# Attention and experts on one core: the last 1024 queries in two groups of 512 instead of four of 256

## The chip, the core and the metric

The kernel runs on one core of a Trainium2 chip. Its engines work side by side, each through its own instruction stream in order, and meet only at semaphores: TensorE (PE, with its weight loads as PEld), VectorE (DVE), ScalarE (ACT), GpSimd (POOL) and SyncE (SP), which starts most DMAs. The metric is the device time of one execution in microseconds (us). A profiled execution also has a span, from its first to its last recorded work.

## The reference

```python
x = L0_attn_x                                   # (1, 2048, 128)
xn = _layernorm(x, axis=-1)
x = x + attention(xn) + ffn(xn)
# attention: one softmax(q k^T * scale) v over all 2048 keys, then a projection
qkv = jnp.einsum('bse,he->bsh', x, w_qkv); q, k, v = jnp.split(qkv, 3, axis=-1)
probs = jax.nn.softmax(jnp.einsum('bqh,bkh->bqk', q, k) * scale, axis=-1)
out = jnp.einsum('bqk,bkh->bqh', probs, v)      # then swapaxes, reshape, w_proj, + b_proj
# ffn: 8 experts (128 -> 512 -> 128), each token in its best two
topv, topi = jax.lax.top_k(softmax(t @ W_gate + b_gate), 2)
mid = relu(einsum('nd,edh->neh', t, W1) + b1); eout = einsum('neh,ehd->ned', mid, W2) + b2
out = einsum('ne,ned->nd', route, eout) @ W_out + b_out
```

## The kernel before, in words

The 2048 tokens stand on 128 partitions as 16 tiles of 128. Attention goes by **groups** of queries (`GROUPS`), here eight of 256. A group goes through the 16 tiles of keys in **steps**. A step fills one bank of PSUM, 512 columns of scores: with 256 queries that is two tiles of keys (`CH` = 2) and 8 steps to a group. With 512 queries it would be one tile of keys and 16 steps, by the same functions.

In a step, PE makes `scores` (each product as three fp32r matmuls, high and low parts), ACT takes the exponential (L454; from group 4 on also an fp32r copy, L453, whose remainder DVE makes, `low`, L611), and two steps later PE sums the values (`values`: L917 in plain fp32 in groups 0 to 3, L926, L927 and L930 as three fp32r products from group 4 on).

The exponentials need each query's maximum first. While one group runs, PE makes the **pairs** of the next group: `pair(g, m)` (L853) is two matmuls of 512 columns for a tile of 128 queries and half of the keys. DVE reduces each to a maximum (`pair_max`, L601, 128x1024 elements). A group has two pairs for each tile of 128 queries. All pairs from group 1 on write the same two banks, so each waits until DVE has read the one before it (`max_read`). `PAIR_STEP[g]` lists the steps of group g at which the pairs of group g+1 stand. If a step has several, the first goes ahead of the step's `values` and the others behind them. When all are read, `row_max` (L606) joins them, and ahead of the group's last step `max_row` (L861) turns them into a row on PE, one transpose for each tile of queries. `q_project` makes the next group's queries in step 0.

After a group, ACT copies the sum out (`copy_u`, L461), and PE and DVE finish it in **rounds** of 256 queries: `out_rows` (L947), `scale_out` (L617, L620), `project` (L961), then one `add_out` for the whole group (L628). `out_rows` of a round waits for the `scale_out` of the one before it, since both use the same bank.

Groups 0 to 3 (`PRE` = 4) run ahead of the **experts**, a loop over 39 tiles of sorted tokens (L1025, L1037, L1051 on PE; L343 on POOL), whose outputs go to `slots_out` in memory. The pairs of group 4 are made in group 3, ahead of the experts. Group 4 and those behind it run after the experts. Beside them POOL gathers the experts' outputs: for each of the 16 tiles of tokens two indirect DMAs (L380) and a multiplication (`weigh`, L375). DVE's `combine(j)` (L756) waits for both and stands at a fixed step s counted from the experts' end (4 + 13(j+1)/8, so j = 15 at s = 30). At s = 14, 22, 26 and 31 (`BLOCK_AT`) PE turns four combined tiles (`moe_transpose`, L1081), and a step later multiplies them with W_out (`moe_project`, L1089); DVE adds that in `moe_add` (L763).

Behind the last step PE has the last `values`, the last `moe_project` and the last group's rounds. SP stores the output in pieces (L277), each when all that is added to its rows is there.

Of the kernel before, what the change touches and what calls it, by code (L numbers as in the profile page):

```python
# [12 lines left out]
def attention_moe_kernel(nc, x, w_qkv, w_proj, b_proj, w_in, b_in, w_gate, b_gate,  # L13
# [4 lines left out]
    P = 128  # L18
    S, D = x.shape[1], x.shape[2]
    NT = S // P  # L20
    NE, _, DM = w1.shape
    HC = DM // P
    BK = 512
    NR = S // BK
    TB = BK // P
# [10 lines left out]

    GROUPS = [(256 * g, 256) for g in range(8)]
    PRE = 4  # L40
    WHOLE = 4

    PAIR_STEP = [[4, 5, 5, 6]] + 6 * [[1, 2, 4, 5]] + [[]]
    NG = len(GROUPS)
    SIZE = [n for _, n in GROUPS]
    CH = [BK // n for n in SIZE]
    STEPS = [NT // c for c in CH]
# [21 lines left out]
    def pairs_at(g, k):  # L69
        return [m for m, at in enumerate(PAIR_STEP[g]) if at == k]  # L70

# [8 lines left out]
    with ctx:  # L80
# [143 lines left out]
        def _(sp):  # L224
# [45 lines left out]
                store_y(t)  # L270

            ov = out.rearrange("o (p j) e -> p (o j) e", p=P)
            cuts = [TB * r for r in range(NR)] + [GROUPS[NG - 1][0] // P, NT]
            for a, b in zip(cuts, cuts[1:]):
                sp.wait_ge(Z["moe_added"], (b - 1) // TB + 1)
                sp.wait_ge(Z["x_added"], sum(q < P * b for q, _ in GROUPS))
                sp.dma_start(ov[:, a:b, :], x_sb[:, a:b, :]).then_inc(Z["stored"], 16)  # L277
            sp.wait_ge(Z["stored"], 16 * (NR + 1))

        @block.gpsimd  # L280
        def _(pool):
# [51 lines left out]
            def load_experts(first, n):  # L333
                _, values = nc.values_load_multi_w_load_instructions(
                    texp[0:1, first:first + n], engines=[pool.engine], min_val=0, max_val=NE - 1,
                    skip_runtime_bounds_check_because="a count of experts that is clamped to the last one")
                experts.update({first + k: v for k, v in enumerate(values)})
# [190 lines left out]
        def _(dve):  # L528
# [69 lines left out]
            def pair_max(g, m):  # L598
                b = pair_bank(g, m)
                dve.wait_ge(Z["max_done"], FIRST_PAIR[g] + m + 1)  # L600
                dve.tensor_reduce(part_max[:, g % 2, m // 2, m % 2:m % 2 + 1], ps[:, b:b + 2, :], AX.XY,  # L601
                                  ALU.max).then_inc(Z["max_read"], 1)

            def row_max(g):
                dve.wait_ge(Z["max_read"], FIRST_PAIR[g + 1])
                dve.tensor_reduce(neg_max[:, g % 2, 0:TILES[g]], part_max[:, g % 2, 0:TILES[g], :], AX.X, ALU.max,  # L606
                                  negate=True).then_inc(Z["neg_max_ready"], 1)
# [15 lines left out]
            def add_out(g):  # L623
                first = GROUPS[g][0] // P
                at = x_sb[:, first:first + TILES[g], :]
                dve.wait_ge(Z["proj_done"], FIRST_ROUND[g + 1])
                dve.wait_ge(Z["x_biased"], 1 + first + TILES[g])
                return dve.tensor_tensor(at, ps[:, MB, 0:SIZE[g]].rearrange("p (j e) -> p j e", e=D), at, ALU.add)  # L628
# [77 lines left out]
            for g in range(PRE):  # L706
                for k in range(STEPS[g]):
                    for m in pairs_at(g, k):
                        pair_max(g + 1, m)
                    if k == PAIR_STEP[g][-1]:  # L710
                        row_max(g + 1)
# [47 lines left out]
            def moe_add(b):  # L759
                at = x_sb[:, TB * b:TB * (b + 1), :]  # L760
                dve.wait_ge(Z["wo_done"], b + 1)
                dve.wait_ge(Z["x_added"], min(NG - 1, sum(q < BK * (b + 1) for q, _ in GROUPS)))
                dve.tensor_tensor(at, ps[:, MX + 1, :].rearrange("p (j e) -> p j e", e=D), at, ALU.add).then_inc(Z["moe_added"], 1)  # L763

            for g in range(PRE, NG):
                for k in range(STEPS[g]):
                    i = FIRST[g] + k
                    s = i - BASE_B
                    for m in pairs_at(g, k):
                        pair_max(g + 1, m)  # L770
                    if g + 1 < NG and k == PAIR_STEP[g][-1]:
                        row_max(g + 1)
# [16 lines left out]
        def _(pe):  # L789
# [287 lines left out]
            def moe_transpose(b, pairs):  # L1077
                pe.wait_ge(Z["c_ready"], TB * (b + 1))
                pe.wait_ge(Z["max_read"], pairs)
                for j in range(TB):  # L1080
                    last = pe.transpose(ps[:, MX, P * j:P * (j + 1)], z[:, TB * b + j, 0, :], ident[:, 0:P])  # L1081
                last.then_inc(Z["cT_done"], 1)
# [9 lines left out]
            for g in range(PRE, NG):  # L1092
                for k in range(STEPS[g]):
# [9 lines left out]
                    if s in BLOCK_AT:  # L1103
                        moe_transpose(BLOCK_AT[s], FIRST_PAIR[g + 1] + sum(at <= k for at in PAIR_STEP[g]))
                    if s - 1 in BLOCK_AT:
# [40 lines left out]
```

## Time and profile before

| | before |
|---|---|
| median of 3 runs | 242.5 us (242.16 to 242.7) |
| profiled execution, its own time | 242.35 us |
| its span | 240.6 us |
| TensorE (PE) busy | 226.1 us, 94% |
| VectorE busy | 136.6 us, 57% |
| ScalarE busy | 111.7 us, 46% |
| GpSimd busy | 140.9 us, 59% |
| granted TensorE clock, mean | 0.998 |

The profiled execution took 1.75 us more than its span, and 0.15 us less than the median of the runs. Shares of busy time are means over parts with different limits, so the table alone doesn't tell what a change in one part is worth. The clock is given as a share of full speed. In the rows further down, a time in square brackets is how long the engine had been idle before the instruction, with what ended the wait.

### The profile page before, as it was taken

The numbers are of one execution on the slowest core, as the hardware profiler recorded it, in microseconds if no ns is written. First come the engines' busy times: TensorE is split into PE (matmuls) and PEld (weight loads), VectorE is DVE, ScalarE is ACT, GpSimd is POOL, SyncE is SP. The second block draws the span as 40 slices with busy tenths as digits, with TensorE's granted clock in tenths as the row PEclk, the third lists the DMA queues.
The fourth block names the chain that finished last, engine by engine and source line by source line (L and its number), as shares of the span: only waits on it lengthen the run. The fifth ranks groups of instructions, "written<-read, shape, count | busy, mean of one in ns | idle before, by whom it ended". The sixth has DMA issues, their size and how long they took to land.

```text
span 240.6 us, 4828 instructions
## 1 busy us (share of the span) xinstructions
PE 226.1 (94%) x1724; PEld 214.0 (89%) x1724; DVE 136.6 (57%) x330; ACT 111.7 (46%) x265; POOL 140.9 (59%) x163
## 2 busy tenths in 40 slices
PE   7699977999999999899999999999899999999983
PEld 7688865889999998899999999999899899999983
DVE  4978585364252551445444445444677886985642
ACT  2572520433524325354444554444656656567561
POOL 3149007888888820266555666553088888888610
PEclk9999999999999999999999999999999999999999
DMA  6799911101111121022222222221111113113201
GB/s 180 282 324 341 322 31 46 45 33 46 46 41 39 43 66 44 14 55 76 70 73 71 67 71 75 69 75 38 33 46 34 44 35 82 40 40 83 75 15 44
DMA packets 23047, 19.54 MB, mean 81 GB/s; under 512 B 3280, under 2 KB 19696, under 8 KB 22768
## 3 DMA queue, kind: packets, MB, share of 16 engines
q1 hardware_dynamic: 20000, 14.71, 20.1%
q0 software_dynamic: 2048, 4.20, 6.5%
q10 hardware_dynamic: 976, 0.33, 0.5%
q8 instruction: 14, 0.23, 0.4%
q14 instruction: 9, 0.07, 0.1%
HBM read 10.97 MB, written 8.26 MB: 80 GB/s over the span
## 4 chain that ended last, share of the span: by engine, by line
PE 78%; DVE 8%; DMA 4%; POOL 3%; issue 2%; ACT 1%; ACTq 1%; POOLq 0%; DVEq 0%
PE ps L1051 15%; PE ps L1037 15%; PE ps L917 10%; PE ps L853 6%; PE ps L792 5%; PE ps L793 5%; PE ps L794 5%; DVE part_max L601 3%; PE ps L926 2%; POOL wtab L380 2%; PE ps L930 2%; PE ps L927 2%; DMA w_raw<-in_L_attn_w_proj_dram 2%; PE ps L1025 2%; PE ps L800 2%
## 5 line engine op out<-in xcount | busy, mean ns | idle before, releaser
L343 POOL COPY wst<-wtab 128x1156 f32 x39 | 45.0, 1154 | 39.3 <-DVE y_sb L738 39.3
L454 ACT ACTIVATE pf<-ps 128x512 f32<-128x512 f32 x64 | 38.1, 595 | 36.5 <-PE ps L794 36.1
L601 DVE TENSOR_REDUCE part_max<-ps 128x1 f32<-128x1024 f32 x32 | 38.9, 1223 | 13.3 <-PE ps L853 13.1
L380 POOL DMA_INDIRECT wtab<-slots_out,slots x32 | 34.4, 1074 | 15.9 <-DMA slots_out<-y_sb 8.4
L353 POOL DMA_INDIRECT slots_in<-hl,slots x32 | 31.5, 985 | 18.7 <-DVE slots L677 11.7
L730 DVE TENSOR_SCALAR mid<-ps,wst 128x128 f32<-128x128 f32 x78 | 23.8, 347 | 32.5 <-PE ps L1037 32.5
L1051 PE MATMUL ps<-wst,mid 128*128 128x128 f32 x312 | 41.3, 275 | 0.7 <-DVE x_sb L628 0.7
L792 PE MATMUL ps<-q_hi,xnT_hi 128*128 128x256 f32 x128 | 41.2, 322 | 0.5 <-ACT q_hi L439 0.5
L1037 PE MATMUL ps<-xgT,wst 128*128 128x128 f32 x312 | 41.3, 275 | 0.0
L1051 PEld LDWEIGHTS ps<-wst,mid 128*128 128x128 f32 x312 | 38.0, 192 | 0.8 <-ACT mid L494 0.8
L1037 PEld LDWEIGHTS ps<-xgT,wst 128*128 128x128 f32 x312 | 38.0, 192 | 0.1
L793 PE MATMUL ps<-q_hi,xnT_lo 128*128 128x256 f32 x128 | 36.1, 282 | 0.0
L794 PE MATMUL ps<-q_lo,xnT_hi 128*128 128x256 f32 x128 | 36.0, 281 | 0.0
L917 PE MATMUL ps<-pf,xn 128*128 128x256 f32 x128 | 32.7, 379 | 0.0
L453 ACT ACTIVATE ph<-ps 128x512 fp32r<-128x512 f32 x32 | 19.1, 598 | 23.4 <-PE ps L794 23.1
L611 DVE TENSOR_TENSOR pl<-pf,ph 128x512 fp32r<-128x512 f32 x32 | 22.6, 706 | 12.2 <-ACT pf L454 12.2
L494 ACT ACTIVATE mid<-ps,wst 128x128 f32<-128x128 f32 x78 | 24.4, 364 | 7.5 <-PE ps L1037 7.5
L917 PEld LDWEIGHTS ps<-pf,xn 128*128 128x128 f32 x128 | 23.0, 189 | 3.1
L487 ACT ACTIVATE xgT<-ps 128x128 f32<-128x128 f32 x39 | 10.9, 278 | 31.8 <-PE ps L1025 31.8
L792 PEld LDWEIGHTS ps<-q_hi,xnT_hi 128*128 128x128 f32 x128 | 24.3, 190 | 1.3 <-ACT q_hi L439 0.7
L853 PE MATMUL ps<-xnT_hi,q_hi 128*128 128x512 f32 x64 | 21.2, 416 | 4.3 <-DVE part_max L601 3.8
L793 PEld LDWEIGHTS ps<-q_hi,xnT_lo 128*128 128x128 f32 x128 | 24.3, 190 | 0.6
(145 smaller groups left out, 341.4 us busy)
## 6 DMA issues: line engine op xcount, KB each, us to landing
wtab<-in_L_ffn_W_dram SPq DMA_DIRECT2D x16, 256.0 KB, 5.9
xg<-slots_in SPq DMA_DIRECT2D x39, 64.0 KB, 2.0
slots_out<-y_sb SPq DMA_DIRECT2D x39, 64.0 KB, 1.5
slots_in<-wst SPq DMA_DIRECT2D x2, 1024.0 KB, 5.0
x_sb<-in_L_attn_x_dram SPq DMA_DIRECT2D x4, 256.0 KB, 4.9
out_dram<-x_sb SPq DMA_DIRECT2D x3, 256.0 KB, 2.6
wtab<-in_L_ffn_b_dram SPq DMA_DIRECT2D x1, 512.0 KB, 7.4
slots_in<-hl,slots POOLq DMA_INDIRECT x32
```

The source lines that it names most:

```text
L343: pool.tensor_copy(wst[:, t % 4, :], wtab[:, bass.ds(experts[t], 1), :].rearrange("p a n -> p (a n)")).then_inc(Z["staged"], 1)
L353: pool.indirect_dma_start(out=slots_in, out_offset=bass.IndirectOffsetOnAxis(ap=slots[:, c, j:j + 1], axis=0), in_=hl[:, j, 0:D], in_offse ...
L380: pool.indirect_dma_start(out=z[:, j, c, :], out_offset=None, in_=slots_out, in_offset=bass.IndirectOffsetOnAxis(ap=slots[:, c, j:j + 1], ...
L454: act.activation(pf[:, i % 3, :], ps[:, st_bank(i), :], ACT.Exp).then_inc(Z["pf_done"], 1)
L601: dve.tensor_reduce(part_max[:, g % 2, m // 2, m % 2:m % 2 + 1], ps[:, b:b + 2, :], AX.XY, ALU.max).then_inc(Z["max_read"], 1)
L792: pe.matmul(dst, lh, rh, start=start, stop=False)
L793: pe.matmul(dst, ll, rh, start=False, stop=False)
L794: return pe.matmul(dst, lh, rl, start=False, stop=stop)
L853: last = pe.matmul(ps[:, pair_bank(g, m) + b, :], q_hi[:, g % 2, P * t:P * (t + 1)], xnT_hi[:, at:at + BK], start=True, stop=True)
L917: last = pe.matmul(dst, xn[:, c, :], pf[:, i % 3, cols(g, h)], start=(first and h == 0), stop=(final and h == CH[g] - 1))
L1037: last = pe.matmul(ps[:, 2 * (t % 2) + h, SL * (c % 2):SL * (c % 2 + 1)], wst[:, t % 4, P * c:P * (c + 1)], xgT[:, t % 2, :], start=True, ...
L1051: last = pe.matmul(ps[:, y_bank(t), 0:D], mid[:, t % 2, c, :], wst[:, t % 4, DM + D * c:DM + D * (c + 1)], start=(c == 0), stop=(c == HC - 1))
```

## The change

The four groups of 256 behind the experts become two of 512. Groups 4 and 5 then have one tile of keys to a step, 16 steps, eight pairs and two rounds each. Group 4's eight pairs stand in group 3's eight steps, ahead of the experts, where four stood. Group 5's eight stand in group 4. The output is stored in four pieces of 512 rows, where the last 512 rows were two pieces.

```diff
-    GROUPS = [(256 * g, 256) for g in range(8)]
+    GROUPS = [(256 * g, 256) for g in range(4)] + [(1024, 512), (1536, 512)]
     PRE = 4
     WHOLE = 4
 
-    PAIR_STEP = [[4, 5, 5, 6]] + 6 * [[1, 2, 4, 5]] + [[]]
+    PAIR_STEP = [[4, 5, 5, 6]] + 2 * [[1, 2, 4, 5]] + [[1, 2, 2, 3, 4, 4, 5, 6], [1, 3, 5, 6, 8, 9, 11, 12], []]
```
```diff
-            cuts = [TB * r for r in range(NR)] + [GROUPS[NG - 1][0] // P, NT]
+            cuts = [TB * r for r in range(NR + 1)]
             for a, b in zip(cuts, cuts[1:]):
                 sp.wait_ge(Z["moe_added"], (b - 1) // TB + 1)
                 sp.wait_ge(Z["x_added"], sum(q < P * b for q, _ in GROUPS))
                 sp.dma_start(ov[:, a:b, :], x_sb[:, a:b, :]).then_inc(Z["stored"], 16)
-            sp.wait_ge(Z["stored"], 16 * (NR + 1))
+            sp.wait_ge(Z["stored"], 16 * NR)
```

First place: PE in group 3, from the pair at step 2 on. L853 is a pair, L917 the values, L947 `out_rows`, L792 to L794 the scores. Before:

```order
L853 MATMUL ps<-xnT_hi,q_hi 128x512 x2
L917 MATMUL ps<-pf,xn 128x256 x2
L947 MATMUL ps<-wvT,ut 128x130 x2
L792 MATMUL ps<-q_hi,xnT_hi 128x256
L793 MATMUL ps<-q_hi,xnT_lo 128x256
L794 MATMUL ps<-q_lo,xnT_hi 128x256
L792 MATMUL ps<-q_hi,xnT_hi 128x256
L793 MATMUL ps<-q_hi,xnT_lo 128x256
L794 MATMUL ps<-q_lo,xnT_hi 128x256
L917 MATMUL ps<-pf,xn 128x256 x2
L961 MATMUL ps<-wpT,o_sb 128x128 x2
```

The same place now:

```order
L853 MATMUL ps<-xnT_hi,q_hi 128x512 x2
L917 MATMUL ps<-pf,xn 128x256 x2
L853 MATMUL ps<-xnT_hi,q_hi 128x512 x2
L947 MATMUL ps<-wvT,ut 128x130 x2
L792 MATMUL ps<-q_hi,xnT_hi 128x256
L793 MATMUL ps<-q_hi,xnT_lo 128x256
L794 MATMUL ps<-q_lo,xnT_hi 128x256
L792 MATMUL ps<-q_hi,xnT_hi 128x256
L793 MATMUL ps<-q_hi,xnT_lo 128x256
L794 MATMUL ps<-q_lo,xnT_hi 128x256
L853 MATMUL ps<-xnT_hi,q_hi 128x512 x2
L917 MATMUL ps<-pf,xn 128x256 x2
```

A second pair stands behind the values of step 2, and one more in step 3.

Second place: PE's last instructions, from the last steps' values on. Before:

```order
L926 MATMUL ps<-ph,xn_hi 128x256
L927 MATMUL ps<-ph,xn_lo 128x256
L926 MATMUL ps<-ph,xn_hi 128x256
L927 MATMUL ps<-ph,xn_lo 128x256
L930 MATMUL ps<-pl,xn_hi 128x256 x2
L1089 MATMUL ps<-wo_sb,cT 128x128 x4
L947 MATMUL ps<-wvT,ut 128x130 x2
L961 MATMUL ps<-wpT,o_sb 128x128 x2
```

Now:

```order
L926 MATMUL ps<-ph,xn_hi 128x512
L927 MATMUL ps<-ph,xn_lo 128x512
L930 MATMUL ps<-pl,xn_hi 128x512
L1089 MATMUL ps<-wo_sb,cT 128x128 x4
L947 MATMUL ps<-wvT,ut 128x130 x2
L961 MATMUL ps<-wpT,o_sb 128x128 x2
L947 MATMUL ps<-wvT,ut 128x130 x2
L961 MATMUL ps<-wpT,o_sb 128x128 x2
```

A step's values are three matmuls of 512 columns instead of six of 256, and the last group has two rounds.

Third place: DVE's last instructions, from the last `combine` (L756) on. Now:

```order
L756 SCALAR_TENSOR_TENSOR wtab<-wtab,gate 128x128
L611 TENSOR_TENSOR pl<-pf,ph 128x512
L763 TENSOR_TENSOR x_sb<-ps,x_sb 128x512
L617 RECIPROCAL rinv<-ps 128x2
L620 TENSOR_TENSOR o_sb<-ps,rinv 128x256
L617 RECIPROCAL rinv<-ps 128x2
L620 TENSOR_TENSOR o_sb<-ps,rinv 128x256
L628 TENSOR_TENSOR x_sb<-ps,x_sb 128x512
```

Before, L617 and L620 stood there once and L628 had 128x256 elements. POOL's instructions are the same, in the same order.

## Rows read from the trace of the kernel before

**Rows 1.** The page: the chain that ended last, by engine.
```profile
PE 78%; DVE 8%; DMA 4%; POOL 3%; issue 2%; ACT 1%; ACTq 1%; POOLq 0%; DVEq 0%
```
**Rows 2.** Windows (us: busy us and count by engine, clock, DMA, GB/s), group 3.
```profile
77.32:92.56 15.24, 15.24 (x97) 13.96 (x96) 6.50 (x9) 6.05 (x11) 7.46 (x8) 1.00 0.21 61
```
**Rows 3.** Timeline of PE in group 3: start us, length us, instruction.
```profile
79.15 0.28 PE L794 MATMUL ps<-q_lo,xnT_hi 128*128 128x256 f32 x1
79.27 0.62 PE L853 MATMUL ps<-xnT_hi,q_hi 128*128 128x512 f32 x2
79.73 1.02 PE L917 MATMUL ps<-pf,xn 128*128 128x256 f32 x4
...
81.30 0.64 PE L853 MATMUL ps<-xnT_hi,q_hi 128*128 128x512 f32 x2
...
84.66 0.61 PE L961 MATMUL ps<-wpT,o_sb 128*128 128x128 f32 x4
85.02 0.36 PE L792 MATMUL ps<-q_hi,xnT_hi 128*128 128x256 f32 x1
...
85.81 0.62 PE L853 MATMUL ps<-xnT_hi,q_hi 128*128 128x512 f32 x2
...
87.85 0.64 PE L853 MATMUL ps<-xnT_hi,q_hi 128*128 128x512 f32 x2
...
90.76 0.38 PE L861 MATMUL ps<-ident,neg_max 128*128 128x128 f32 x2
...
92.56 0.27 PE L1025 MATMUL ps<-ident,xg 128*128 128x128 f32 x1
```
**Rows 4.** Timeline of DVE in group 3.
```profile
79.93 1.23 DVE L601 TENSOR_REDUCE part_max<-ps 128x1 f32<-128x1024 f32 x1 [1.08 <-PE ps L853]
...
89.78 0.16 DVE L606 TENSOR_REDUCE neg_max<-part_max 128x2 f32<-128x4 f32 x1
```
**Rows 5.** Timeline of POOL behind the experts: first gather, three later ones, last weigh.
```profile
173.99 1.47 POOL L380 DMA_INDIRECT wtab<-slots_out,slots  x1 [8.37 <-DMA slots_out<-y_sb]
...
187.34 1.00 POOL L380 DMA_INDIRECT wtab<-slots_out,slots  x1 [0.17 <-issue]
...
190.44 1.00 POOL L380 DMA_INDIRECT wtab<-slots_out,slots  x1 [0.17 <-issue]
...
197.45 1.46 POOL L380 DMA_INDIRECT wtab<-slots_out,slots  x1 [0.17 <-issue]
...
228.58 0.60 POOL L375 TENSOR_SCALAR wtab<-wtab,gate 128x128 f32<-128x128 f32 x1 [1.10 <-DMA wtab<-slots_out,slots]
```
**Rows 6.** Timeline of DVE behind the experts.
```profile
187.28 0.39 DVE L756 SCALAR_TENSOR_TENSOR wtab<-wtab,gate 128x128 f32<-128x128 f32 x1 [0.25 <-POOL wtab L375]
...
197.36 0.68 DVE L611 TENSOR_TENSOR pl<-pf,ph 128x512 fp32r<-128x512 f32 x1
...
231.51 0.34 DVE L756 SCALAR_TENSOR_TENSOR wtab<-wtab,gate 128x128 f32<-128x128 f32 x1
```
**Rows 7.** Waits from 169 us on: engine, line, releaser: total us, times, longest.
```profile
PE ps L853 <- DVE part_max L601: 1.1, 2, 0.6
```
**Rows 8.** Timeline of PE and DVE at the end.
```profile
235.44 0.68 PE L947 MATMUL ps<-wvT,ut 128*128 128x130 f32 x4
235.64 0.69 DVE L763 TENSOR_TENSOR x_sb<-ps,x_sb 128x512 f32<-128x512 f32 x1 [2.61 <-PE ps L1089]
...
236.92 0.71 PE L961 MATMUL ps<-wpT,o_sb 128*128 128x128 f32 x4 [0.80 <-DVE o_sb L620]
237.72 0.42 DVE L628 TENSOR_TENSOR x_sb<-ps,x_sb 128x256 f32<-128x256 f32 x1 [0.86 <-PE ps L961]
```
**Rows 9.** All copies of line 461: ns min/median/max, first and last start.
```profile
L461 ACT ACTIVATE ut<-ps x8: 603/618/634, 48.6 to 234.7; 128x256 f32<-128x256 f32 x8
```
**Rows 10.** DMA issues: KB each, median us to landing.
```profile
out_dram<-x_sb SPq DMA_DIRECT2D x3, 256.0 KB, 2.6
out_dram<-x_sb SPq DMA_DIRECT2D x2, 128.0 KB, 2.0
```

## Prediction, written before the result

> **What bounds the kernel now.** I read the chain of work that ended last first: PE holds 78% of it [rows 1]. So the kernel is a stream of matmuls, and I asked of each of three stretches what stands on PE's path there: group 3 ahead of the experts, the steps behind the experts, and the end.
>
> In group 3, PE is busy for 15.24 of 15.24 us [rows 2]. Nothing waits there now: a pair follows the one before it by 2.03 us or more (79.27 to 81.30), and DVE's reading fits in between [rows 3, 4].
>
> Behind the experts there is a second stream that nobody on PE or DVE feeds: POOL's gathers. They start at 173.99, once the experts' last output has landed, and the last `weigh` ends at 228.58 + 0.60 = 229.18 [rows 5]. That is 55.19 us, 3.45 for each of 16 tiles. The last `combine` stands at 231.51 [rows 6], so POOL is only 2.33 us ahead of what needs it. Early on it is already late once: at 187.28 DVE had been idle for 0.25 us on POOL. This decides the case: whatever PE saves behind the experts, the last `combine` can come 2.33 us earlier and no more, unless POOL gets quicker too.
>
> **Group 3 and the start of the experts.** Four pairs more, and eight readings in a row. Prices: a matmul of 256 columns 0.12 (79.15 to 79.27), a pair 0.46 (79.27 to 79.73), so 0.23 for 512 columns. The 2.03 us from pair to pair are 0.46, six score matmuls (0.71) and the values, 0.86. After plain fp32 work the scores take 0.79 (85.02 to 85.81), and a `project` 0.36 (84.66 to 85.02), which I also take for `out_rows`. A pair may start when the one before is read: 0.66 to DVE's start, 1.23 for the maximum and about 0.06 to PE, 1.95 in all [rows 3, 4].
>
> Counted from the first pair: second 2.03. Third, in the same step: PE is there at 3.35, the reading allows 3.98, wait 0.63. Fourth: PE 3.98 + 0.46 + 0.36 + 0.79 = 5.59, allowed 5.93, wait 0.34. Fifth: 5.93 + 0.46 + 0.86 + 0.36 + 0.79 = 8.40, no wait. Sixth: PE 9.72, allowed 10.35, wait 0.63. Seventh: PE 10.35 + 0.46 + 0.71 = 11.52, allowed 12.30, wait 0.78. Eighth: 14.33, no wait. The joining of the maxima ended 89.78 + 0.16 = 89.94, 2.09 behind the last pair at 87.85, so `max_row` can start at 14.33 + 2.14 = 16.47, where PE stands at 15.65: wait 0.82. From `max_row` to the experts were 1.80 us (90.76 to 92.56), two more transposes add about 0.14: 18.41. Before, it took 92.56 - 79.27 = 13.29. With 0.33 more for a `q_project` of 512 columns (three times 0.23 instead of 0.12), the experts start **5.5 us later**: 1.84 of matmuls, 3.2 of waits, 0.47 of wider steps. Bounds: 5.2 if each reading is a tenth quicker, 6.0 if it is a tenth slower, since PE's first matmul after a wait is longer. The experts' loop doesn't change, so all behind it moves by this.
>
> **Behind the experts.** On PE alone much goes: four pairs (1.84), the two waits on maxima (1.1 [rows 7]), two `q_project` of 0.36 each less the widening of the one that stays (0.4), one round of 0.72, and 0.01 for each of some 186 times that one wide matmul takes the place of two (1.9). Against it stand about 0.1 at each of three places with pairs in neighbouring steps, and some 0.5 where group 5's first values wait for the copy of 512 columns. Together about 5.0 us less.
>
> POOL lets little of this through. Its instructions are the same, its start is tied to the experts' end, so with its old length the last `combine` gains 2.33. Its length is not quite fixed. Where DVE waited for POOL and then ran `combine` (187.28), the next tile's turn took 190.44 - 187.34 = 3.10 us against 3.45 in the mean; that is to be the usual state now, and 14 tiles at 3.10 would save 4.9. Where DVE's `low` had started just ahead of a gather (197.36 and 197.45), the gather took 1.46 instead of 1.00. Seven of the 16 first gathers were over 1.3 us; if all were, the chain would be 9 x 0.4 = 3.6 longer. So the last `combine` gains between -1.3 and the 5.0 that PE allows. I take **3.3 earlier**, nearer to the old length, since only one such turn was measured beside a pace of 3.45.
>
> On this the Trainium skill has a rule (SBUF — State Buffer, "SBUF: two separate sides"): VectorE and GpSimd share a pair of ports under an exclusive lock, and a VectorE operation with two SBUF inputs takes it only against a GpSimd operation that reads SBUF. The trace agrees that the two hold each other up, but with 1.46 beside `low` the gather's issue suffers as well. By the rule's letter only the 16 `weigh` could grow and shrink, and the sum would stay near a gain of 2.3.
>
> **The end.** From the last `combine` to the last `project` the work is PE's values (the same columns), `moe_project` and the rounds. (a) The copy L461 takes 0.62 for 256 columns [rows 9]; for 512 between that and twice that, on the path: +0.3. (b) The second round: its `out_rows` stands behind the first round's `project` (0.46 with its start after a wait), and from `out_rows` to `project` are 236.92 - 235.44 = 1.48 [rows 8]: +1.94. (c) `add_out` with 512 columns as `moe_add`, 0.69 instead of 0.42: +0.27. (d) the last store has 256 KB, landing in 2.6 instead of 2.0 [rows 10]: +0.6. Together **3.1 later**, between 2.5 and 3.7. The stores no longer overlap with this end, since the rows 1536 to 1791 now belong to the last group.
>
> **Sum.** 5.5 - 3.3 + 3.1 = 5.3 us more than the profiled execution: span 245.9, time 247.65. The median of the runs shown stood 0.15 above the profiled execution, which is within their spread; I forecast 247.7.
>
> **Rivals.**
> - POOL's chain keeps its length or grows by up to 1 us: 5.5 - 2.3 + 3.1 = 6.3, so 248.7, up to 249.7. For it: the instructions are the same. I count it with the forecast; together they are "POOL sets the end", 246.7 to 249.7.
> - PE sets the end, because POOL's turns shrink to 3.10: 5.5 - 5.0 + 3.1 = 3.6, so about 246.0. For it speaks the turn at 187.34, against it that it is one turn.
> - Collisions: POOL now starts each tile at the moment at which DVE is released, and `low` falls on the first gather each time: up to 3.6 more, 250 to 252.3. Against it: at 187.28 it was `combine` that came first, and that gather took 1.00.
> - Faster than before: POOL's turns go to the shortest pieces, and nothing on PE is later. The point from which it decides: 5.5 + 3.1 - 2.33 = 6.3 us must go from the chain, so 48.9 us for 16 tiles, 3.06 a tile, below the quickest turn that rows show. At 2.97 (two gathers of 0.95 with their gaps and a `weigh` of 0.6) it would be 1.4 below before, 241.0, and PE would have to be 10 us shorter too.
>
> For that last condition there is a rule. The Trainium skill (TensorE: Matmul & The Clock Gate, "Back-to-back issue gap") gives a sustained 131 ns for a matmul of 512 columns. An estimate from that page: against 0.24 for two narrow ones, 186 times, some 20 us less on PE. The pair in group 3 with 0.23 for 512 columns speaks against it, and even by the rule POOL's chain would keep the end where it is.
>
> **How the numbers follow.** POOL sets the end, 246.7 to 249.7: 0.62. PE sets the end, 245.3 to 246.7: 0.18. Collisions, 249.7 to 252.3: 0.14. Faster: 0.02; about as before, by a chain near 49 us: 0.01; the rest, 0.03, lies between 243 and 245.3. The range 245.6 to 250.4 leaves out about 2 in 10. A measurement of this kernel can tell about 0.2% from no change, 0.5 us. Faster 0.02, same 0.01, slower 0.97.
>
> **What would show it.** In the trace of after: the experts' first transpose (L1025) near 98.1 instead of 92.56, with PE's waits on L601 in group 3 summing to about 2.4 us and one of 0.8 on L606; DVE waiting for `weigh` at most of the `combine`s, the last `combine` within 0.1 us of the last `weigh`'s end; POOL's first gather at about 179.5, and its chain between 51 and 56 us; two rounds at the end and 8.7 + 3.1 us from the last `combine`'s turn on. The prediction is wrong if the readings in group 3 hide behind PE's work, or if POOL's chain turns out not to be independent of the others.

## The result, and the profile after

The changed kernel takes **249.88 us** (median of four runs, 249.47 to 250.34), the kernel before 242.41 us (242.16 to 242.70, four runs beside them). The ratio is 1.031, with a 95% interval of 1.0285 to 1.0333. The change costs 7.5 us; 5.3 were forecast, and the range of 245.6 to 250.4 us holds the result.

The profiled execution, the slowest of the four, has a span of 248.4 us against 240.6, so +7.8. The four runs of after differ in their spans: 248.4, 248.4, 247.0 and 246.8 us, with times of 250.34, 250.13, 249.64 and 249.47 us. So two runs have 1.5 us less of span, but only 0.7 us less of time: their time exceeds the span by 2.6 to 2.7 us, that of the others by 1.7 to 1.9. Why isn't in the records. The sums below go by the span of the profiled execution.

From the page of after, the chain that ended last by engine, and the granted clock in 40 slices:

```profile
PE 59%; POOL 17%; DVE 10%; issue 6%; DMA 3%; ACT 1%; ACTq 1%; POOLq 0%; DVEq 0%
...
PEclk9999999999999999999999999999999999999979
```

PE held 78% of the chain before [rows 1] and holds 59% now. POOL went from 3% to 17%, DVE from 8% to 10%. That is two new waits: PE for DVE's readings in group 3, and DVE, and through it PE, for POOL behind the experts. The granted clock shows one slice at 0.7, the last but one.

**Group 3.** The timeline of PE, the first seven of the eight pairs (L853; the eighth starts at 94.33, without a wait), `max_row` (L861) and the experts' first transpose (L1025), to be held against [rows 3]:

```profile
79.56 0.63 PE L853 MATMUL ps<-xnT_hi,q_hi 128*128 128x512 f32 x2
...
81.60 0.64 PE L853 MATMUL ps<-xnT_hi,q_hi 128*128 128x512 f32 x2
...
83.56 0.72 PE L853 MATMUL ps<-xnT_hi,q_hi 128*128 128x512 f32 x2 [0.45 <-DVE part_max L601]
...
85.60 0.73 PE L853 MATMUL ps<-xnT_hi,q_hi 128*128 128x512 f32 x2 [0.16 <-DVE part_max L601]
...
88.18 0.63 PE L853 MATMUL ps<-xnT_hi,q_hi 128*128 128x512 f32 x2
...
90.13 0.73 PE L853 MATMUL ps<-xnT_hi,q_hi 128*128 128x512 f32 x2 [0.45 <-DVE part_max L601]
...
92.18 0.73 PE L853 MATMUL ps<-xnT_hi,q_hi 128*128 128x512 f32 x2 [0.60 <-DVE part_max L601]
...
96.57 0.62 PE L861 MATMUL ps<-ident,neg_max 128*128 128x128 f32 x4 [0.74 <-DVE neg_max L606]
...
98.61 0.27 PE L1025 MATMUL ps<-ident,xg 128*128 128x128 f32 x1
```

PE waits at exactly the pairs at which the forecast put a wait (third, fourth, sixth, seventh) and at `max_row`. The experts start at 98.61 instead of 92.56, 6.05 us later. DVE's readings of the sixth and of the eighth pair:

```profile
90.90 1.23 DVE L601 TENSOR_REDUCE part_max<-ps 128x1 f32<-128x1024 f32 x1 [0.82 <-PE ps L853]
...
95.00 1.23 DVE L601 TENSOR_REDUCE part_max<-ps 128x1 f32<-128x1024 f32 x1 [0.82 <-PE ps L853]
```

They are 4.10 us apart, so 2.05 from reading to reading: 1.23 of reading and 0.82 in which DVE waits for the next pair. From a reading's end to the next pair are 0.05 us (90.90 + 1.23 = 92.13, the pair at 92.18).

**Behind the experts.** The timeline of POOL, the first two gathers, a `weigh`, and the last tile, against [rows 5]:

```profile
180.03 1.00 POOL L380 DMA_INDIRECT wtab<-slots_out,slots  x1 [8.36 <-DMA slots_out<-y_sb]
181.34 1.38 POOL L380 DMA_INDIRECT wtab<-slots_out,slots  x1 [0.30 <-issue]
...
188.36 1.05 POOL L375 TENSOR_SCALAR wtab<-wtab,gate 128x128 f32<-128x128 f32 x1
...
230.22 0.95 POOL L380 DMA_INDIRECT wtab<-slots_out,slots  x1 [0.30 <-issue]
...
234.07 0.60 POOL L375 TENSOR_SCALAR wtab<-wtab,gate 128x128 f32<-128x128 f32 x1 [2.24 <-DMA wtab<-slots_out,slots]
```

and the waits of after from 174 us on (engine, line, releaser: total us, times, longest):

```profile
DVE wtab L756 <- POOL wtab L375: 13.1, 13, 2.1
...
PE ps L1081 <- DVE wtab L756: 2.7, 1, 2.7
```

DVE now waits for a `weigh` 13 times in 16. POOL's chain starts 6.04 later and ends at 234.67: 54.64 us instead of 55.19. The last tile's rows land 1.1 us later behind their gather's issue than before (POOL idle for 2.24 instead of 1.10). SP's store of the rows 1024 to 1535 stands beside that gather:

```profile
230.46 0.33 SPq L277 DMA_DIRECT2D out_dram<-x_sb  x1
```

**The end.** The timeline of DVE (last `combine`, `moe_add`, `add_out`) and of PE, against [rows 6] and [rows 8]:

```profile
234.78 0.35 DVE L756 SCALAR_TENSOR_TENSOR wtab<-wtab,gate 128x128 f32<-128x128 f32 x1 [1.29 <-POOL wtab L375]
...
244.74 0.69 DVE L628 TENSOR_TENSOR x_sb<-ps,x_sb 128x512 f32<-128x512 f32 x1 [0.86 <-PE ps L961]
```
```profile
235.19 1.12 PE L1081 MATMUL ps<-ident,wtab 128*128 128x128 f32 x4 [2.70 <-DVE wtab L756]
...
236.53 0.63 PE L927 MATMUL ps<-ph,xn_lo 128*128 128x512 f32 x1
236.96 0.63 PE L930 MATMUL ps<-pl,xn_hi 128*128 128x512 f32 x1
...
238.64 0.39 PE L926 MATMUL ps<-ph,xn_hi 128*128 128x512 f32 x1
238.87 0.39 PE L927 MATMUL ps<-ph,xn_lo 128*128 128x512 f32 x1
...
240.62 0.71 PE L947 MATMUL ps<-wvT,ut 128*128 128x130 f32 x4 [0.24 <-ACT ut L461]
242.05 0.71 PE L961 MATMUL ps<-wpT,o_sb 128*128 128x128 f32 x4 [0.72 <-DVE o_sb L620]
...
243.93 0.71 PE L961 MATMUL ps<-wpT,o_sb 128*128 128x128 f32 x4 [0.72 <-DVE o_sb L620]
```

PE stood still for 2.70 us at L1081, and then values of 512 columns follow one another by 0.43 us (236.53 to 236.96) until 238.24, and by 0.23 from 238.64 on. The windows of these two stretches (us: busy us and count of PE, PEld, DVE, ACT, POOL; clock; DMA; GB/s) give the granted clock, 0.50 and 1.00:

```profile
235.19:238.24 3.05, 3.05 (x10) 2.57 (x11) 0.54 (x1) 0.60 (x1) 0.00 (x0) 0.50 0.00 0
238.64:248.40 9.76, 4.32 (x28) 3.43 (x26) 2.57 (x6) 1.04 (x1) 0.00 (x0) 1.00 0.07 27
```

The first is the level of 1.2 GHz, the second that of 2.4 GHz. So behind that wait the clock was at the lower level for some 3 us.

From the start of the last transposes (235.19) to the end of the span are 13.21 us, where they were 8.69 (240.6 − 231.91). The whole move of the span is then:

| | forecast | measured |
|---|---|---|
| group 3, to the experts' start | +5.5 | +6.05 |
| last `combine`, seen from the experts | −3.3 | −2.78 (234.78 − 231.51 = 3.27; 6.05 − 3.27) |
| the end, without the clock | +3.1 | +3.0 |
| the end, by the clock | not foreseen | +1.5 |
| sum | +5.3 | +7.8 |

The 4.52 us of the two last rows split so: transposes 0.35 and values 1.14 longer (the clock, 1.5 together); 0.41 to the first `out_rows` (the copy of 512 columns); 1.88 for the second round; 0.27 for `add_out`; 0.51 for the larger store; −0.05 in the first round.

### The profile page after: what moved, and what is told of

The parts are those of the page before. It is cut to its first block, busy times and chain, and to the rows that moved or that the text cites. A ratio compares the mean times of both kernels' runs of the same rounds, so it can differ in the third digit from the quotient of the medians.

```text
span 248.4 us, 4409 instructions
## 1 busy us (share of the span) xinstructions
PE 228.2 (92%) x1526; PEld 204.8 (82%) x1526; DVE 136.2 (55%) x324; ACT 111.2 (45%) x259; POOL 139.0 (56%) x163
## 4 chain that ended last, share of the span: by engine, by line
PE 59%; POOL 17%; DVE 10%; issue 6%; DMA 3%; ACT 1%; ACTq 1%; POOLq 0%; DVEq 0%
PE ps L1051 14%; PE ps L1037 14%; POOL wtab L380 13%; PE ps L917 8%; DVE part_max L601 5%; PE ps L853 5%; POOL wtab L375 5%; PE ps L792 3%; PE ps L794 2%; PE ps L793 2%; DMA w_raw<-in_L_attn_w_proj_dram 2%; PE ps L1025 2%; PE ps L800 2%; PE ps L961 1%; PE ps L947 1%
## 5 line engine op out<-in xcount | busy, mean ns | idle before, releaser
L601 DVE TENSOR_REDUCE part_max<-ps 128x1 f32<-128x1024 f32 x32 | 38.9, 1222 | 14.2 <-PE ps L853 12.1
L353 POOL DMA_INDIRECT slots_in<-hl,slots x32 | 31.5, 986 | 18.7 <-DVE slots L677 11.7
L380 POOL DMA_INDIRECT wtab<-slots_out,slots x32 | 32.1, 1003 | 15.9 <-DMA slots_out<-y_sb 8.4
L792 PE MATMUL ps<-q_hi,xnT_hi 128*128 128x256 f32 (+1 forms) x96 | 35.2, 366 | 0.5 <-ACT q_hi L439 0.5
L917 PE MATMUL ps<-pf,xn 128*128 128x256 f32 x128 | 32.8, 379 | 0.0
L794 PE MATMUL ps<-q_lo,xnT_hi 128*128 128x256 f32 (+1 forms) x96 | 30.5, 318 | 0.0
L793 PE MATMUL ps<-q_hi,xnT_lo 128*128 128x256 f32 (+1 forms) x96 | 30.5, 317 | 0.0
L853 PE MATMUL ps<-xnT_hi,q_hi 128*128 128x512 f32 x64 | 21.4, 418 | 5.9 <-DVE part_max L601 5.3
L917 PEld LDWEIGHTS ps<-pf,xn 128*128 128x128 f32 x128 | 23.2, 189 | 3.4
L611 DVE TENSOR_TENSOR pl<-pf,ph 128x512 fp32r<-128x512 f32 x32 | 22.0, 694 | 4.3 <-ACT pf L454 4.0
L792 PEld LDWEIGHTS ps<-q_hi,xnT_hi 128*128 128x128 f32 x96 | 18.2, 189 | 2.3 <-ACT q_hi L439 0.7
L793 PEld LDWEIGHTS ps<-q_hi,xnT_lo 128*128 128x128 f32 x96 | 18.2, 189 | 1.6
```

Of the source, the lines that this page charges most:

```text
L353: pool.indirect_dma_start(out=slots_in, out_offset=bass.IndirectOffsetOnAxis(ap=slots[:, c, j:j + 1], axis=0), in_=hl[:, j, 0:D], in_offse ...
L380: pool.indirect_dma_start(out=z[:, j, c, :], out_offset=None, in_=slots_out, in_offset=bass.IndirectOffsetOnAxis(ap=slots[:, c, j:j + 1], ...
L792: pe.matmul(dst, lh, rh, start=start, stop=False)
L793: pe.matmul(dst, ll, rh, start=False, stop=False)
L794: return pe.matmul(dst, lh, rl, start=False, stop=stop)
L853: last = pe.matmul(ps[:, pair_bank(g, m) + b, :], q_hi[:, g % 2, P * t:P * (t + 1)], xnT_hi[:, at:at + BK], start=True, stop=True)
```

## Experiments

**Theory 1** is that of the prediction: in after, POOL's chain of gathers and `weigh` sets when the last `combine` stands, and in before it did not. Its rival is that the order of work on PE and DVE sets it in both. **Theory 2** is that of the end: about 3 us for wide columns and the second round, 1.5 for the clock. **Theory 3** is that of group 3: PE waits for the readings of eight pairs, and all behind moves by the same amount. (Some of the expectations below call a theory on the stalls of the other engines their theory 2.)

### One wide group: the end undone

```diff
-    GROUPS = [(256 * g, 256) for g in range(4)] + [(1024, 512), (1536, 512)]
+    GROUPS = [(256 * g, 256) for g in range(4)] + [(1024, 512), (1536, 256), (1792, 256)]
...
-    ... [1, 3, 5, 6, 8, 9, 11, 12], []]
+    ... [1, 5, 8, 11], [1, 2, 4, 5], []]
...
```

The edit is shown against the changed kernel. The rows from 1536 on are two groups of 256 again, stored in two pieces.

> Group 4 stays 512 wide with its eight pairs in group 3; the last 512 queries go back to two groups of 256 and the output to five stores. The end's theory (a second round, the wider copy, the wider addition and the bigger last store stand on the path, 3.1 us in the sum and 3.1 us measured without the clock's part): the stretch from the last combine to the end goes back to about 9.1 us where the clock holds and 10.6 where it falls again; the experts still start at 98.6 and the last combine stays at 234.8, since GpSimd's chain sets it. Time 3.0 to 4.5 us below the changed kernel, some 245.5 to 247. Rival, that the width of the groups behind the experts itself costs or saves time there: the last combine moves by a microsecond or more either way.

Measured: 246.62 us (246.10 to 246.84), ratio 1.0169 (1.0151 to 1.0186), span 244.9. Its timelines of DVE and of PE:

```profile
235.79 0.35 DVE L756 SCALAR_TENSOR_TENSOR wtab<-wtab,gate 128x128 f32<-128x128 f32 x1 [0.57 <-POOL wtab L375]
```
```profile
236.20 0.66 PE L1081 MATMUL ps<-ident,wtab 128*128 128x128 f32 x4 [1.39 <-DVE wtab L756]
```

From 236.20 to the end are 8.7 us, the 8.69 of before, and the clock held. So the end of after costs 13.2 − 8.7 = 4.5 us, the clock included. The expectation was wrong on the last `combine`: it stands 1.0 us later than in after, not at the same place, so its gain seen from the experts is only 1.8 us here. POOL's chain started as in after but took 55.6 us: its gathers' issue 0.7 and its `weigh` 0.8 more in sum, its smaller gaps less. So the grouping behind the experts has an effect on POOL's chain too.

### The maxima of group 4 read from a quarter

```diff
-                dve.tensor_reduce(part_max[...], ps[:, b:b + 2, :], AX.XY,
+                read = ps[:, b:b + 2, 0:BK // 4] if g == PRE else ps[:, b:b + 2, :]
+                dve.tensor_reduce(part_max[...], read, AX.XY,
```

> The changed kernel, but of group 4's eight pairs VectorE reads only 256 of 1024 columns for the maximum (the softmax is then shifted by the maximum of a quarter of the keys; all else is computed). Theory, that PE's waits in group 3 are for the reading: a reading takes 0.4 instead of 1.23 us, the waits on L601 (1.7 us) vanish and that on L606 (0.7) mostly, and the experts start near 95.2 to 95.8 instead of 98.6; time down by about 3. Rival, that the pairs cost it on PE (switches between kinds of matmul, weight loads): the experts still start after 97.5.

Measured, one run: 245.64 us, span 243.6. All readings of the kernel, eight of them of a quarter, then the third pair, the experts' start and the last transposes (lines stand one further down):

```profile
L602 DVE TENSOR_REDUCE part_max<-ps x32: 424/1224/1226, 19.2 to 195.4; 128x1 f32<-128x1024 f32 x24, 128x1 f32<-128x256 f32 x8
```
```profile
82.93 0.81 PE L854 MATMUL ps<-xnT_hi,q_hi 128*128 128x512 f32 x2
...
95.31 0.27 PE L1026 MATMUL ps<-ident,xg 128*128 128x128 f32 x1
...
231.89 0.66 PE L1082 MATMUL ps<-ident,wtab 128*128 128x128 f32 x4 [2.68 <-DVE wtab L757]
```

With readings of 0.42 us in place of 1.23 the waits in group 3 are gone, and the experts start at 95.31 instead of 98.61, 3.3 us earlier. The transposes stand at 231.89 instead of 235.19, again 3.3 earlier: all behind group 3 moves with it, as theory 3 has it. The span fell by 4.8. The other 1.5 is the clock: PE was idle for 2.68 us here, as long as in after, and yet the values behind it followed by 0.23. From the transposes to the end are 11.7 us here (243.6 − 231.89), with the same work as in after. That divides the 4.5 us of the end: 3.0 for what theory 2 lists, 1.5 for the clock.

### `weigh` left out, in after and in before

```diff
-                pool.wait_ge(s_z[j], 32)
-                pool.tensor_scalar(z[:, j, 0, :], z[:, j, 0, :], gate1[:, j:j + 1], None, ALU.mult).then_inc(Z["z_weighed"], 1)
...
-                dve.wait_ge(Z["z_weighed"], j + 1)
+                dve.wait_ge(Z["gates_ready"], 1)
```

> The changed kernel without GpSimd's 16 multiplications by the first gate (line 375 left out, so the first expert's share is not weighted); its 32 gathers stay. Theory, that GpSimd's chain holds back what PE saves behind the experts: the chain takes some 43 us instead of 54.6, VectorE's 13 waits at combine go, the last combine comes 2 to 2.5 us earlier against the experts' end (59.6 before it, now about 56.5 to 57.5), PE doesn't wait 2.7 us ahead of the last transposes, the clock stays at full and the time falls by 3 to 4. Rival, that PE's own path is as long: under 0.5.

> The kernel before with the same 16 multiplications left out. Theory: GpSimd was 2.3 us ahead at the end and late only once early on, so it gains 0.3 to 0.8 us, about the 0.6 us that PE waited at 188.86. If it gains as much as the changed kernel does (3 us or more), the chain was the limit in both and the forecast read it wrongly.

Measured, one run each: after without `weigh` 273.45 us, before without it 276.72. Work was taken away, and the kernels became 24 and 34 us slower, which no theory had. Windows of the first (us: busy us and count of PE, PEld, DVE, ACT, POOL; clock; DMA; GB/s), and its timelines of POOL and of DVE and PE:

```profile
200.00:210.00 10.00, 2.75 (x7) 2.17 (x8) 2.78 (x4) 1.08 (x2) 7.78 (x8) 0.55 0.19 52
...
232.00:262.00 30.00, 28.43 (x144) 22.86 (x144) 16.24 (x32) 19.74 (x36) 0.00 (x0) 1.00 0.07 27
```
```profile
204.32 0.94 POOL L379 DMA_INDIRECT wtab<-slots_out,slots  x1 [0.30 <-issue]
205.56 0.94 POOL L379 DMA_INDIRECT wtab<-slots_out,slots  x1 [0.30 <-issue]
```
```profile
205.97 1.23 DVE L600 TENSOR_REDUCE part_max<-ps 128x1 f32<-128x1024 f32 x1 [5.01 <-remote]
...
218.66 1.23 DVE L600 TENSOR_REDUCE part_max<-ps 128x1 f32<-128x1024 f32 x1 [10.87 <-remote]
```
```profile
207.25 1.22 PE L852 MATMUL ps<-xnT_hi,q_hi 128*128 128x512 f32 x2 [9.21 <-issue]
```

POOL issues gather after gather, mostly 1.25 us apart (204.32 to 205.56), without a pause. Some 10 us after the first one (180.23), PE, DVE and ACT begin to stand still for 2 to 11 us at a time, in before up to 23, at waits for many of which the trace shows no cause ("remote", "issue"). PE is busy for 2.75 of 10 us at 200. DVE reads at 205.97 the pair that PE started at 195.93, and at 218.66 the one of 207.25; in after that takes 0.67 us (88.18 to 88.85). From 232 on, some 11 us behind POOL's last gather (220.54), PE is busy for 28.43 of 30 us. The two runs say nothing on theory 1, since the stalls cover whatever POOL's shorter chain gave.

### The wait of `weigh` kept, its multiplication left out

```diff
                 pool.wait_ge(s_z[j], 32)
-                pool.tensor_scalar(z[:, j, 0, :], z[:, j, 0, :], gate1[:, j:j + 1], None, ALU.mult).then_inc(Z["z_weighed"], 1)
...
-                dve.wait_ge(Z["z_weighed"], j + 1)
+                dve.wait_ge(Z["gates_ready"], 1)
```

> The changed kernel with the 16 multiplications left out again, but with GpSimd's 16 waits for a tile's landing kept where they stood (the first expert's share is not weighted). Theory 1, that GpSimd's chain holds back what PE saves: a tile takes about 2.6 us instead of 3.4, the last combine comes 2 to 3 us earlier against the experts' end, PE's wait of 2.7 us ahead of the last transposes goes, and the span falls by 3 to 4 us from 248.4. Theory 2, that the stalls of the run without multiplications come from gathers issued without a pause: they are gone here, since the waits pace them. Rival: stalls of several us stay, so they come from something else than a missing pause.

> The kernel before with the same edit. Theory 1: GpSimd was ahead except once, so the span falls by 0.3 to 0.8 us from 240.6. Rival: it falls by 3 us or more, so the chain was the limit in both kernels.

Measured, one run each: 273.96 and 276.63 us. The waits didn't pause POOL: a tile's rows had landed by the time its turn came, and the gathers stayed 1.25 us apart in most places (180.09 to the last end near 221.6). The stalls stayed with them, so theory 1 is again not tested, and that the waits would pace the gathers was wrong. The stalls don't come from POOL running ahead of its data; they come with 32 gathers issued without other work between.

### `weigh` on 16 of its 128 columns

```diff
-                pool.tensor_scalar(z[:, j, 0, :], z[:, j, 0, :], gate1[:, j:j + 1], ...
+                pool.tensor_scalar(z[:, j, 0, 0:16], z[:, j, 0, 0:16], gate1[:, j:j + 1], ...
```

> The changed kernel, but GpSimd multiplies 16 of the 128 columns (112 columns of the first expert's share are not weighted). Theory 1, that the gather chain holds back what PE saves: each of the 16 multiplications is about 0.4 us shorter, the last combine comes 2 to 3 us earlier against the first gather (54.75 now), limited by PE, and the span falls by 3 to 4 us from 248.4 with the clock's part. Theory 2, that the stalls of 27 us come as soon as no GpSimd instruction but gathers runs, and not from the pace: with the short multiplication in place they are gone. Rival to 2, that the pace alone brings them: at 2.9 us a tile, between 2.5 with stalls and 3.2 without, some stalls appear and the span grows.

> The kernel before with the same narrow multiplication. Theory 1: GpSimd was ahead of its need but for one place, so the span falls by 0.3 to 0.8 us from 240.6. Rival: it falls by 3 us or more and the chain was the limit in both.

The rest of the first expert's share stays unweighted. Measured, one run each. After: 246.43 us, span 244.4. Its timelines of POOL and DVE:

```profile
180.26 0.99 POOL L380 DMA_INDIRECT wtab<-slots_out,slots  x1 [8.36 <-DMA slots_out<-y_sb]
...
228.24 0.35 POOL L375 TENSOR_SCALAR wtab<-wtab,gate 128x16 f32<-128x16 f32 x1
230.22 0.33 POOL L375 TENSOR_SCALAR wtab<-wtab,gate 128x16 f32<-128x16 f32 x1 [1.63 <-DMA wtab<-slots_out,slots]
```
```profile
232.38 0.34 DVE L756 SCALAR_TENSOR_TENSOR wtab<-wtab,gate 128x128 f32<-128x128 f32 x1
```

A `weigh` takes mostly 0.35 instead of 0.62, and nothing else was changed. The last `combine` comes 52.1 us behind the first gather instead of 54.75, DVE doesn't wait for POOL there any more, and the span falls by 4.0 us (with the 1.5 of the clock, which held). So in after POOL's chain did set the end: theory 1 holds for after, by this one run. With that limit away the last `combine` stands 232.38 − 180.26 = 52.12 behind the first gather, against 231.51 − 173.99 = 57.52 before: a gain of 5.4, near the 5.0 that the prediction gave PE alone. It is not quite PE's own limit, though, since DVE has idle time without a cause here too, which was 0.2 us in after:

```profile
DVE pl L611 <- issue: 2.9, 4, 1.6
```

Before, with the same edit: 247.80 us, 5.4 **slower** than before itself (its span 5.5 longer). POOL's chain is shorter, but the last `combine` stands later:

```profile
224.89 0.33 POOL L375 TENSOR_SCALAR wtab<-wtab,gate 128x16 f32<-128x16 f32 x1 [0.95 <-DMA wtab<-slots_out,slots]
```
```profile
236.96 0.35 DVE L756 SCALAR_TENSOR_TENSOR wtab<-wtab,gate 128x128 f32<-128x128 f32 x1
```

In its waits from 174 us on, more of that idle time has appeared, where before itself has none:

```profile
DVE pl L611 <- issue: 6.0, 6, 2.5
```

Theory 1 and its rival don't have this. Of the expectations for the run of after only the rival on the stalls foresaw it, that the pace of the gathers alone brings some. It looks like the stall of the runs without `weigh` in a milder form. A tile's turn on POOL is 2.5 us in the runs without `weigh` and the stalls cost 24 to 34 us; here it is (224.89 + 0.33 − 173.99) / 16 = 3.2 on average and 2.8 in undisturbed turns, and they cost about 5. After has the same turns (3.1 on average) and came near what PE allows, so the pace alone doesn't say what a kernel loses. So that POOL was not the limit in before rests on the rows (DVE waited for a `weigh` twice in the stretch, 0.6 us in all) and was not shown by a run.

### The store of rows 1024 to 1535 put off

```diff
             for a, b in zip(cuts, cuts[1:]):
...
+                if a == 2 * TB:
+                    sp.wait_ge(Z["c_ready"], NT)
```

> The changed kernel, but the store of rows 1024 to 1535 waits until the last combine is done. Theory: that store of 256 KB, started at 230.46 beside the last gather (230.22), made the gather land 1.1 to 1.2 us late, since GpSimd waited 2.24 us for it where it waited 1.10 before; the last combine comes 1.1 us earlier, PE's wait falls from 2.7 to 1.6 us, and the time falls by 1.1 us, and by up to 1.4 more if the clock then holds at the end. Rival, that the gather is slow for another reason: no change in the last combine. The moved store could also meet the last one, which would cost up to 0.5.

Measured: 247.84 us (247.70 to 249.95), ratio 1.0251 (1.0204 to 1.0298), span 246.0. SP's store is now at 234.31. Timelines of POOL and DVE (lines two further down):

```profile
230.12 0.95 POOL L382 DMA_INDIRECT wtab<-slots_out,slots  x1 [0.30 <-issue]
...
232.64 1.13 POOL L377 TENSOR_SCALAR wtab<-wtab,gate 128x128 f32<-128x128 f32 x1 [0.92 <-DMA wtab<-slots_out,slots]
```
```profile
233.88 0.35 DVE L758 SCALAR_TENSOR_TENSOR wtab<-wtab,gate 128x128 f32<-128x128 f32 x1 [0.49 <-POOL wtab L377]
```

From the last gather's issue to the last `weigh` are 2.52 us, where after had 234.07 − 230.22 = 3.85. With a store within 0.6 us behind that issue the kernel with one wide group shows 4.18 (230.78 to 234.96), that with the quarter read 3.91 and that with the late transposes (next section) 3.94; with both late edits, the store away again, it is 2.59. So the store of 256 KB held the last gather's data back by about 1.3 us. The last `combine` gained 0.9 of it, since this `weigh` took 1.13 beside DVE's work, and by its spans the clock held in three of four runs (246.0, 246.2 and 246.0, against 247.9). In the profiled one PE waited 1.80 us for the last `combine`.

### The last transposes behind the next values

```diff
-                    if s in BLOCK_AT:
+                    if s in BLOCK_AT and s != LAST - 1 - BASE_B:
                         moe_transpose(...
...
             values(LAST - 2)
+            moe_transpose(NR - 1, FIRST_PAIR[NG])
```

> The changed kernel, but PE's last four transposes stand behind the values of steps 29 and 30 instead of ahead of them; all is computed. Theory, that the wait for the last combine costs so much because 1.4 us of PE's work is queued behind it: PE's wait falls from 2.7 to about 1.3 us and the time by 1.4 us, and by 1.4 more where the clock no longer falls. Rival, that the order at the end doesn't matter because ScalarE's copy of the transposed tiles and of the sums comes last: less than 0.5.

> The kernel before, all of it computed, with PE's last four transposes behind the values of steps 29 and 30. PE waited 0.73 us there for the last combine with 1.4 us of work queued behind it, so the time falls by 0.7 us, to about 241.7 (ratio 0.997). Rival, that the copies at the end come last and take the gain: no change within 0.2 us.

> The changed kernel with both late edits (the transposes behind two steps' values, the store of rows 1024 to 1535 behind the last combine). Theory, that they are two terms of one wait (2.7 us, of which 0.9 by the store's contention and 1.6 coverable by PE's work): the last combine at 233.9, a wait of some 0.3 us, span about 244.6, 3.8 below the changed kernel with the clock's 1.4. What then stays over the kernel before, 4.0 us, is the 6.0 of the experts' later start less what the chain lets through plus the second round. Rival, that they don't add: span as with one of them, 245.5.

Measured: after with this edit 247.47 us (247.22 to 247.81), ratio 1.0211 (1.0193 to 1.0230). The transposes wait for less, and the clock held in its profile, by the spans (245.4 and 245.5) in all four runs:

```profile
235.05 0.66 PE L1081 MATMUL ps<-ident,wtab 128*128 128x128 f32 x4 [1.13 <-DVE wtab L756]
```

After with both this and the late store: 246.51 us (246.44 to 247.05), ratio 1.0176 (1.0161 to 1.0192); the wait is down to 0.34:

```profile
234.43 0.66 PE L1083 MATMUL ps<-ident,wtab 128*128 128x128 f32 x4 [0.34 <-DVE wtab L758]
```

So 3.4 us of the 7.5 come back by two edits in the order: 2.4 by the transposes (wait and clock), 1.0 more by the store. 4.1 us are left. They fit group 3 and the longer end less what the last `combine` gained, but no run undoes all of these together.

Before with the late transposes: 241.64 us (241.54 to 241.90), ratio 0.9971 (0.9960 to 0.9982), as expected. It is 0.8 us faster than before, and the fastest of all kernels here: the old grouping, with its last transposes one step later.

## Why the prediction was right, and where its sizes were off

**Group 3: mechanism right, size 0.55 too small.** Each wait stands where the count put it. The reading from a quarter shows that the waits come from the readings, and that they are worth 3.3 us, where the count had 3.2. (The brackets on L601 sum to 1.66 and not to the 2.4 that the prediction named, because a bracket starts at the modelled end of the matmul before, 0.17 or so behind the point from which the count goes.) What was too small is the price of a pair. All were taken at 0.46; the four behind a wait take 0.56 to 0.57 (83.56 to 84.12), and the time to the next pair is longer by 0.1 each, whether DVE sets it (92.18 − 90.13 = 2.05, counted 1.95) or PE (88.18 − 85.60 = 2.58, counted 2.47). The rest is 0.1 at `max_row` and 0.1 behind it. The prediction blamed PE's first matmul after a wait for its upper bound of 6.0, and the result is just above that. The wait is not the only cause: in the kernel with the quarter read the third pair follows the values at once and takes 0.65 (82.93 to 83.58).

**Behind the experts: mechanism right, gain 2.8 instead of 3.3.** POOL's chain became the limit: DVE waits for a `weigh` 13 times, where it did twice, and a shorter `weigh` makes after faster. The chain went from 55.19 to 54.64 us. The gathers' issue became 2.3 shorter, the direction in which the prediction leaned. The group of all 32 gathers on POOL reads in after:

```profile
L380 POOL DMA_INDIRECT wtab<-slots_out,slots x32 | 32.1, 1003 | 15.9 <-DMA slots_out<-y_sb 8.4
```

Only one of them is long (1.38 at 181.34), where seven were over 1.3 us before. (The prediction called all seven first gathers of their tile. One, at 195.26, was a second one; its bound for collisions moves little by that. It also had POOL late once in before, where the waits show two, of 0.6 us in sum.) Why so few are long now isn't shown by a run. Against these 2.3 us stand 0.35 for longer `weigh`, 1.1 for the last landing and 0.3 in gaps between instructions. The last landing was the step that was missed: the prediction moved the store of rows 1024 to 1535 and priced it only at the very end, not as a neighbour of the last gather. The late store shows the price. In before, the matching store was issued 1.4 us behind the last gather (227.25 and 225.87), in after 0.24. At 1.4 us it cost little: 2.71 us from issue to use, against 2.52 with no store there.

On POOL and DVE holding each other up: where `low` started at 188.25, the `weigh` at 188.36 took 1.05 us, and others without it 0.60 to 0.63. The gather at 181.34, beside a `low`, took 1.38. The Trainium skill (SBUF — State Buffer, "SBUF: two separate sides") has VectorE operations with two SBUF inputs lock the shared ports against a GpSimd operation that reads SBUF. The `weigh` agrees with it: all that took 0.77 us or more have a `low` beside them. Whether the issue of a gather, which takes its row numbers from `slots`, counts as such an operation the page doesn't say. The prediction read it as if it didn't, so that the gain would have stayed near 2.3; it was 2.8, and what moved was the gathers.

**The end: 3.0 instead of 3.1, near in each term.** Copy 0.41 (forecast 0.3), second round 1.88 (1.94), `add_out` 0.27 (0.27), store 0.51 (0.6). With one wide group the end is as long as before, 8.7 us.

**The clock: not foreseen.** The prediction had DVE wait for POOL and left PE's wait at L1081 out of account: the clock stands in its sum at nothing, without a reason. A wait of 2.7 us there was followed by the lower clock, which cost 1.5 us of span in transposes and values. By the spans it fell in two of after's four runs (248.4 against 246.8 and 247.0), and in one of the four with the late store. It did not fall in the profiled execution with the quarter read (idle 2.68), nor, the runs with stalls aside, in the other profiled ones of wide groups, with waits of 1.80, 1.39, 1.13, 0.81 and 0.34 us. What tips it isn't settled here.

**Luck in the number.** The measured 249.88 lies outside the 246.7 to 249.7 of "POOL sets the end", the case that came, and inside the band of the collisions, which didn't come. The range holds it because it reached into that band. Of the 2.2 us between the forecast 5.3 and the measured 7.5, group 3 has 0.55, the last `combine` 0.5, and the rest is largely the clock.

**Rivals.** "PE sets the end" fell: its 246.0 needed turns of 3.10 us from the start. The last four turns do take 3.1 to 3.2 (225.82 to 228.91 is 3.09), but the nine before them 3.1 to 3.65, so the mean stays at 3.4. "Collisions" fell: one long gather, not sixteen. The rule of 131 ns for a matmul of 512 columns (the Trainium skill, TensorE: Matmul & The Clock Gate, "Back-to-back issue gap") is not seen here either: 0.23 us from 238.64 to 238.87. "Faster" needed a chain of 48.9 us; it was 54.64. That it would be slower was right for the reason given: of the work taken off PE behind the experts, about half was cover for POOL's chain and not the path to the end.

## What to carry to other kernels

When an edit takes work from the engine that is busiest, look for the stream of another engine that ends just ahead of the same join, and measure its slack. Here it was 2.3 us, and of some 5 saved on PE (5.4 with the narrow `weigh`) only 2.8 arrived. Then count every reading and every store that the edit moves: readings in a row turn from hidden to exposed once their turn-around (2.05 us here) is longer than PE's work between two of them, and a large store beside the last gather delays it (1.3 us here).

## What the runs showed of the hardware

- **With gathers issued without a break the other engines stall.** With 32 of them 1.25 us apart PE, ACT and DVE stood still for up to 11 us at a time in one kernel and up to 23 in the other, and the kernels took 24 to 34 us longer. With 2.8 us for two gathers and a narrow `weigh`, one kernel lost about 5 us, and the other had 2.9 us of unexplained idle time on DVE; with the whole `weigh`, 3.1 us and more, it is 0.2 us or none. Taking work off POOL can thus make a kernel slower. The records show only that an engine can go on some 9 us after the work it waits for (a pair of 195.93, 0.73 us long, read at 205.97); whether a signal is late or something else isn't in them.
- **A wait of 2.7 us on PE brought the lower clock level in some executions and not in others**, at the same place of the same program: the granted clock was 0.50 from 235.19 to 238.24.
- **A store of 256 KB beside an indirect gather of 64 KB** put the gather's landing off by about 1.3 us (3.85 to 4.18 from issue to use with the store 0.2 to 0.6 us behind, 2.52 and 2.59 with none there).
